# Window attention, convolution and MLP block on one core: values as fp32 weights with ones columns, one K/Q array for both score passes, unrolled code, a new order on every engine, long matmuls as two 64-column halves

## The reference, cut to what matters

```python
xn = layernorm(xw, g, b)                       # per token over 96 channels
q, k, v = split(xn @ qkv_w.T + qkv_b)          # 12 heads of 8
attn = softmax(q * SCALE @ k.T + bias)         # 49 x 49, per window and head
seq = x + (attn @ v) @ proj_w.T + proj_b       # back in image order
bn = batchnorm(depthwise_conv3x3(seq))         # inference constants
out = bn + gelu(bn @ w1.T + b1) @ w2.T + b2    # 96 -> 384 -> 96
```

## Time and profile before

| what | value |
|---|---|
| three runs | 4437.77, 4467.01, 4476.71 us |
| median | 4467.01 us |
| span of the profiled execution (its own time) | 4483.3 us, 16 us above the median |
| busy in it: TensorE, VectorE, ScalarE, GpSimd | 4149.9, 4035.2, 3540.7, 1813.2 us |
| instructions | 143736 |
| DMA issued by SP | 329.89 MB |

### The profile page before, as it was taken

One profiled execution on the slowest core, in us unless ns is written; L12 is line 12 of the kernel. 1 busy time (PEld: TensorE's weight loads), 2 busy tenths in 40 slices (PEclk: granted clock), 3 DMA queues, 4 the chain that ended last, 5 costly groups with the idle time before them and its releaser, 6 DMA issues.

```text
span 4483.3 us, 143736 instructions
## 1 busy us (share of the span) xinstructions
PE 4149.9 (93%) x51980; PEld 2703.3 (60%) x51980; DVE 4035.2 (90%) x7480; ACT 3540.7 (79%) x5891; POOL 1813.2 (40%) x1559
## 2 busy tenths in 40 slices
PE   4999999999999999999999999999999999999998
PEld 2666666666666666666666666666666666666665
DVE  6799999889999999998999899999999998988997
ACT  2688887878878788878888788788788888787886
POOL 3334444444343434434443434344343443434442
PEclk9899999999999999999999999999999999999998
DMA  1222222222222222222222222222222222222221
GB/s 48 69 76 81 77 78 76 78 78 81 77 77 77 77 78 80 76 78 75 80 81 76 79 76 78 76 81 78 76 78 77 80 76 80 75 79 77 80 79 41
DMA packets 363523, 340.69 MB, mean 76 GB/s; under 512 B 67200, under 2 KB 362561, under 8 KB 362708
## 3 DMA queue, kind: packets, MB, share of 16 engines
q1 hardware_dynamic: 362708, 329.89, 25.5%
HBM read 39.48 MB, written 38.54 MB: 17 GB/s over the span
## 4 chain that ended last, share of the span: by engine, by line
DVE 38%; issue 26%; PE 18%; SPq 11%; DMA 4%; ACT 2%; DVEq 1%; ACTq 0%; POOL 0%; POOLq 0%
DVE s L808 11%; DVE mx L777 6%; SPq L278 5%; DVE rec L790 4%; DMA q_bd<-ql 3%; DVE vl L844 3%; DVE on L794 3%; SPq L276 2%; PE a_ps L517 2%; DVE y L838 2%; SPq L319 2%; PE st_ps L368 2%; DVE kl L817 2%; DVE ol L856 2%; PE st_ps L362 2%
## 5 line engine op out<-in xcount | busy, mean ns | idle before, releaser
L680 POOL TENSOR_TENSOR pl<-p,ph 128x588 f16<-128x588 f32 x1024 | 1349.1, 1317 | 1890.5 <-ACT ph L584 1890.5
L808 DVE SCALAR_TENSOR_TENSOR s<-ximg,cols,s 96x392 f32<-96x392 f32 x2048 | 1610.6, 786 | 98.2 <-issue 71.4
L777 DVE TENSOR_REDUCE mx<-sm_ps 128x12 f16<-128x588 f32 x1024 | 780.8, 763 | 126.1 <-PE sm_ps L383 118.5
L581 ACT ACTIVATE p<-st_ps 128x588 f32<-128x588 f32 x1024 | 673.4, 658 | 184.9 <-PE st_ps L368 162.6
L584 ACT ACTIVATE ph<-st_ps 128x588 f16<-128x588 f32 x1024 | 681.9, 666 | 0.0
L517 PE MATMUL a_ps<-g,w_s 128*96 128x392 f32 x1536 | 618.2, 512 | 0.0
L336 PE MATMUL o_ps<-vh,ph 128*128 128x36 f16 x6144 | 559.9, 182 | 1.8 <-POOL pl L680 1.7
L337 PE MATMUL o_ps<-vl,ph 128*128 128x36 f16 x6144 | 551.0, 180 | 0.0
L338 PE MATMUL o_ps<-vh,pl 128*128 128x36 f16 x6144 | 551.0, 180 | 0.0
L336 PEld LDWEIGHTS o_ps<-vh,ph 128*128 128x128 f16 x6144 | 487.3, 96 | 53.2 <-POOL pl L680 2.3
L368 PE MATMUL st_ps<-q_bd,k_st 113*64 113x98 f16 x12288 | 484.3, 214 | 34.0 <-issue 34.0
(11 more groups left out here) (131 smaller groups left out, 8347.0 us busy)
## 6 DMA issues: line engine op xcount, KB each, us to landing
q_st<-qm SPq DMA_DIRECT2D x512, 96.0 KB
q_bd<-qh SPq DMA_DIRECT2D x1024, 48.0 KB
k_st<-kh SPq DMA_DIRECT2D x512, 96.0 KB
x_sb<-in_x SPq DMA_DIRECT2D x256, 147.0 KB, 2.3
out<-y SPq DMA_DIRECT2D x256, 147.0 KB, 2.4
k_bd<-kh SPq DMA_DIRECT2D x512, 48.0 KB
k_st<-kl SPq DMA_DIRECT2D x256, 96.0 KB
q_bd<-ql SPq DMA_DIRECT2D x512, 48.0 KB
```

The lines of the kernel that those rows point to most:

```text
L581: af(p32[:, q % 2, :, :].rearrange("p (b h) n -> p b h n", b=2), src, ACT.Exp)
L680: tt(pl[:, p % 2, :, 0:TOK], p32[:, p % 2, :, :], ph[:, p % 2, :, 0:TOK], ALU.subtract).then_inc(pl_done, 1)
L777: v.tensor_reduce(mx[:, (st[1] - lag) % 2, :, p].rearrange("p (b h) -> p b h", b=2), sm_ps[:, :, 0:HALF].rearrange("p b (h n) -> p b h n", ...
L808: v.scalar_tensor_tensor(acc, image_rows(st, lag, k // 3, k % 3), cw_c[:, k:k + 1], acc, ALU.mult, ALU.add)\
```

## The change

- All steps are written out (`for s in range(STEPS)`, 266 of them); every semaphore target is a constant. Many semaphores are split by pass.
- `k_all` and `q_all` (128 rows: rows 0 to 31 hold the three terms of a head's 8 channels, every fourth row a term; the rows behind them, and three spare ones, are one-hot for the keys in `k_all` against the bias's high and low part in `q_all`; row 127 takes the maximum) serve both passes. The maximum pass uses rows 0 to 126. SP issues nine DMAs a step.
- Both passes: 24 matmuls of 49 columns per pair of windows, each with 49 weight columns in one 64-partition half. L362, `qm`, `k_bd`, `q_st` are gone.
- One exponential, fp32. `values_times_p` has V as fp32 weights: 32 columns per head and pair of windows, column 4d+0 and 4d+1 the value for either window, 4d+2 and 4d+3 ones, so that the output has O and the sums, channels first, in a 32-partition group. V is written by one VectorE product with a 0/1 table (`half_c`).
- ScalarE copies O out; GpSimd issues four DMAs that gather every fourth partition into `ox`; ScalarE turns the sums into 1/sum as exp(-ln sum); VectorE multiplies; the projection is fp32 with its bias added in `image_sum`. Transposes, `oh` and `ol` are gone.
- `wide`: every matmul with over 64 output channels is issued as two, each with 64 weight columns (96 channels are padded to 128).

```diff
-                for b in range(2):
-                    mm(st_ps[:, b, 0:HALF], hot2[:, :, :].rearrange("p a b -> p (a b)"), lo_l[:, b * HALF:(b + 1) * HALF],
-                       start=True, stop=False, skip_group_check=True)
-                for j in range(NJ):
+                for h in range(HEADS):
                     for w in range(2):
-                        n = (2 * q + w) * WP
-                        c0 = j % (NJ // 2) * 2 * TOK
-                        last = mm(st_ps[64 * w:64 * w + 64, j // (NJ // 2), c0:c0 + 2 * TOK], k_st[:, r, j, n:n + WP],
-                                  q_bd[:, r, 2 * j:2 * j + 2, n:n + TOK], start=False, stop=True, skip_group_check=True)
+                        n, c0 = (2 * p + w) * WP, h % HH * TOK
+                        last = mm(st_ps[64 * w:64 * w + TOK, h // HH, c0:c0 + TOK], k_all[:, r, h, n:n + TOK],
+                                  q_all[:, r, h, n:n + TOK], start=True, stop=True)
...
+            def wide(o, w, m, start=True, stop=True):
+                for h in range(2):
+                    last = mm(o[64 * h:64 * h + 64], w[:, 64 * h:64 * h + 64], m, start=start, stop=stop)
+                return last
...
+                for g3 in range(NG):
+                    for c4 in range(4):
+                        h, at = 4 * g3 + c4, (2 * g3 + p % 2) * TOK
+                        last = mm(o_ps[32 * c4:32 * c4 + 32, at:at + TOK], v32[:, c % 2, h, p, :], p32[:, p, h, :], start=True, stop=True)
...
+            def to_channels(c):
...
+                wait(pool, proj_done, c - 2)
+                wait(pool, o_done[0], c)
+                wait(pool, o_done[1], c)
...
+                for x4 in range(4):
+                    nc.gpsimd.dma_start(ox[:, c % 2, x4, :], o_sb[x4::4, c % 2, :, :]).then_inc(o_in[c % 2], 16)
```

More of the change, by code:

```diff
@@ L325, in _, with load, term @@
-            run(sp, step)
+            def load(c):
+                if not real(c):
+                    return
+                wait(sp, sum_done, c - CPI)
+                at = c % CPI * CT
+                sp.dma_start(x_sb[:, at:at + CT], dram_rows(x, c)).then_inc(x_in[c % 8], 16)
+            def term(t, n, part, done, c):
+                if not real(c):
+                    return
+                wait(sp, done, c)
+                sp.dma_start(t[n:TERMS:4, c % 4, :, :], part[:, c % 2, :]).then_inc(exp_in[c % 4], 16)
@@ new lines, in store @@
+            def store(c):
+                if not real(c):
+                    return
+                wait(sp, y_done, c)
+                sp.dma_start(dram_rows(out, c), y[0:C, c % 2, :]).then_inc(stored[c % 2], 16)
+            for s in range(STEPS):
+                first_term(k_all, 1, kl, kl_done, s - 3)
+                load(s)
+                term(k_all, 0, kh, kh_done, s - 3)
+                term(q_all, 0, qh, qh_done, s - 3)
+                term(q_all, 1, qh, qh_done, s - 3)
+                term(q_all, 2, ql, ql_done, s - 3)
+                term(k_all, 2, kh, kh_done, s - 3)
+                store(s - 10)
+                maximum_row(s - 4)
@@ L457, in values, with projection @@
                 last.then_inc(v_done, 1)
-            def channels_first(st):
-                if not real(st, 4):
+            def projection(c):
+                if not real(c):
                     return
-                wait(pe, norm_done, st, 4, 4)
-                if real(st, 0):
-                    wait(pe, lnv_done, st, 0)
-                else:
-                    wait(pe, y_done, st, 8)
-                for n in range(NP):
-                    last = nc.tensor.transpose(a_ps[0:C, n * 128:(n + 1) * 128], on[:, n, :], eye_f[:, :])
-                last.then_inc(ot_ps_done, 1)
@@ L472, in projection @@
[L472 to L486 removed]
+                wait(pe, norm_done, c)
@@ new lines, in second @@
+            def second(c, k):
+                if not real(c):
+                    return
+                wait(pe, g_done[k], c)
+                if k == 1:
+                    free(pe, (g_done[2], c+0), (sum_done, c+2), (lnv_done, c+7), (y_done, c-1))
+                wide(a_ps[0:128, 0:CT], w2_s[:, k, :], g[:, k, :], start=k == 1, stop=k == 2).then_inc(s_done[k], 1)
+            for s in range(STEPS):
+                hidden(s - 8, 0)
+                hidden(s - 8, 1)
+                maxima_rows(s - 3)
+                hidden(s - 8, 2)
+                max_scores(s - 2, 0)
+                exp_scores(s - 4, 3)
+                values_times_p(s - 4, 1)
+                values_times_p(s - 4, 0)
+                second(s - 8, 1)
+                keys(s - 1)
+                max_scores(s - 2, 1)
+                second(s - 8, 0)
+                second(s - 8, 2)
+                queries(s - 1)
+                exp_scores(s - 3, 0)
+                values_times_p(s - 4, 2)
+                values_times_p(s - 4, 3)
+                max_scores(s - 2, 2)
+                centred(s)
+                values(s - 2)
+                exp_scores(s - 3, 1)
+                variance(s)
+                max_scores(s - 2, 3)
+                exp_scores(s - 3, 2)
+                projection(s - 5)
@@ L893 @@
     w_qkv, b_qkv, w_proj = a(L0_conv_qkv_w), a(L0_conv_qkv_b), a(L0_conv_proj_w).T
+    low = np.zeros((ROWS, 1), np.float32)
+    for row, key, n in LOW:
+        low[row:row + n] = -1.0
+    half = np.zeros((128, 2), np.float32)
+    for w in range(2):
+        half[64 * w:64 * w + TOK, w] = 1 / UP
     col = lambda v: a(v).reshape(C, 1)
@@ L910 @@
         "eye": np.eye(128, dtype=np.float32),
+        "low": low, "half": half,
     }
```

913 lines of the change are left out of this document (393 added, 520 removed).

## The result

The changed kernel takes 3539.8 us (median of 4 runs, 3533.4 to 3545.4) against 4471.9 for the one before on the same chip: 0.7918 of its time, with a 95% interval of 0.7885 to 0.7951. It is the number of rival D (3540), by coincidence: D had TensorE without waits, and it does wait.

The account below looks back on a forecast made before the run. Neither TensorE nor VectorE alone was taken as the bound. From 4483.3 us: -180 loop, -485 steps (16.3 to 14.4 us), -15 fill, +10 short last steps, -16 to the median: 3795 us, range 3610 to 3980.

Parts of the forecast that it names:

- rival D: TensorE runs its list without waits: 13.4 us a step, 3540 us in all; chance 0.05.
- Loop: Writing out all steps removes 30 back edges of 6.0 us: 180 us less, with straight code priced at 0.
- rival C: Gain only partly had, through weight loads (44 ns a pair), fetch or late results: 15.2 to 16.3 us a step; chance 0.17.
- TensorE, P times V: 48 fp32 matmuls a step at about 47 ns plus four shape changes: 2.65 us, range 2.25 to 4.3, against 1.83.
- fp32 halves: Long fp32 matmuls on TensorE, issued as two overlapping halves, still cost 0.66 us each, with results 0.33 us later.
- projection: On TensorE, two fp32 matmuls of 196 columns without transposes: 0.75 us a step against 1.92.
- GpSimd's issues: GpSimd issues four DMAs itself, at 1.0 us each, out of 0.7 to 2.5.
- what I cannot see: Allowance of 0.4 us a step for unseen costs, added to 13.3 of TensorE work and 0.7 of waits.
- Rival A: The fp32 halves on TensorE do not overlap: 21.9 us a step, about 5780 us in all; chance 0.08.
- B: GpSimd's transfers hold ScalarE, deciding the step from 1.46 us an issue; up to 18.2 us a step, about 4790; chance 0.11.
- VectorE and ScalarE: Busy time a step falls from 15.96 to 12.1 us on VectorE and from 13.9 to 10.9 on ScalarE.
- SP: SP issues nine DMAs for 18; nothing waited long for it, so no gain was counted there.

Follow-up runs that it names:

- the fastest version: Changed kernel with SP issuing the keys' terms first and the load behind all terms, and O's four transfers moved from GpSimd to SP: 3397.6 us, 0.7601.

## Why the prediction was wrong

*Loop:* right, 168 for 180, in a run of its own. The price of straight code was put at nothing, with the rest in rival C. For the list before that holds. In the changed kernel's denser list TensorE stands 0.54 us a step in issue, most of it in holes that go with the fetching of instructions (last section).

*TensorE, P times V:* the term that was mis-sized. It took 2.65 us a step, out of 2.25 to 4.3, "about 47 ns a matmul, plus four changes of shape"; it is 1.32, under the lower end. The working gave the overlap to one record of each matmul, by the halves of L368. There are four column groups, and the order turns through all four. Its 41 ns a record held (43 within a group), but four groups do this at once: 22 ns a matmul, 27 with the change of shape. The bound was no bound, since it let at most two groups overlap. 1.33 x 255 = 339 us, more than the whole miss.

*fp32 halves, projection, GpSimd's issues:* the times are right or better (0.66 to 0.68; 0.69 for 0.75; 0.57 us for 1.0). The order of the halves was read wrongly: they do not follow one another shifted by one record, both start together (7 ns apart), so the results are not 0.33 later. The 0.3 us a step named for that stands in the sum only as far as "what I cannot see" holds it. Rival A is refuted by the timeline, B by 9.6 us of waits in the whole run, C's pairs of 44 ns by 27; C's other half, fetch, did take its 0.5 us a step.

*VectorE and ScalarE:* right, 11.85 for 12.1 and 11.24 for 10.9. Taps are 619 ns for 0.62.

*SP:* the step that was missing. "Nothing waited long for SP, so nothing is gained there" asked only what SP gives back, not what hangs on it afterwards. In the changed kernel six issues of 0.7 us and the load stand between the keys and the next maximum pass, and a landing of 3.0 to 3.6 behind them. With 3.9 us ahead of them this closes at 12.9, more than TensorE's 11.8. The sum held 1.1 us of waits, 0.7 of them named (ScalarE's exponential, the logarithm) and 0.4 "for what I cannot see"; it was 13.29 - 11.82 = 1.5. In the trace 1.05 of that are gaps of over 0.1 us: 0.41 for the keys' transfer, 0.54 in issue, 0.09 ahead of the projection, and next to nothing for the exponential.

*Sum:* steps of 13.29 for 14.4 are -283 us, the fill is 141 for 168, -27; the short last steps take some of it back, and so do the 16 us taken off for the profiled execution, which here lies 4 us under the median. The reasons for the direction held. The size came out of two errors of opposite sign: a list 1.5 us a step too long, 1.33 of it in a term whose own range was too narrow, and waits 0.4 too short.

## What to carry to other kernels

When a change adds copies or transfers between the place where something is made and the place of its next use, draw that chain round to its own start and add it up (issues in their order, landing, work on both sides); compare it with every engine's list, however idle the queue looks before. An order on the issue queue costs nothing to change: here, to put the terms that the next step waits for ahead of the load was worth 108 us, and another queue for four other transfers 34 more. And when work turns through four parallel parts of an engine, the lower bound of its cost is the cost in one part divided by four, until a row shows that fewer overlap.

## What the runs showed of the hardware

**Column groups.** Twenty-four fp32 matmuls of 49 columns with 32 weight columns take 0.66 us when they turn through the four column groups, and 1.20 us when three in a row go to one group. Within a group a record takes 43 ns in both; the difference is how many groups run at once, four or two.

**Landing.** The last of the six terms lands 3.0 us after its issue's end where GpSimd's first transfer is issued together with it (the kernel after, the second layer's product twice), and 1.9 to 2.0 where that comes 0.6 us later or more (the order of P times V, the centred product twice, keys first); medians from the packets. In all of these SP sends a load or a store right behind, so 2.0 is not the landing of a transfer alone. That GpSimd's transfers are the reason is read from this order of the runs; none left them out. The Trainium skill, "SBUF — State Buffer", Who interferes with whom, has GpSimd's descriptors starve while VectorE holds the shared port. GpSimd's 1024 issues took 0.56 to 0.73 us each, and no such thing shows; but the instructions that the page names for it (copies, casts, tensor_scalar) are not those that ran beside them in the step shown (products, maxima, sums), so this is no test of it.

**Holes without a releaser.** TensorE stands still for up to 2.0 us (2.3 with two key terms on GpSimd) at places where it waits for nothing shown. From the chain of the kernel after:

```profile
2022.85 0.38 PE b_ps L250 x18
2023.23 1.62 issue
2024.85 0.31 PE b_ps L250 x6
```

Counted from the records between 300 and 3200 us, gaps over 0.8 us that are put to issue: 71 (86 us) in the kernel after, 75 (93) with the keys first, 76 (93) in the fastest version, all of them at the 194th or 195th instruction of a block of 256 in TensorE's list; 19 (20) when the fastest has a product more, and 4 (6) with whole products and the keys first. The page of the kernel after has 742 packets with 12.16 MB on the instruction queue, 16.4 KB each, and 742 blocks of 256 are TensorE's instructions. In these three runs every hole ends 1.1 to 1.7 us after the end of such a packet; of moments taken at random some 13% do. So TensorE waits there for its next block of instructions, as far as records can tell: no run changed the fetching alone. The runs do show that these holes pay for added work: 169 us of a product more arrived as 91, and the holes shrank by 73 in 2900 us. By the same account whole products would have cost some 260 us instead of 157 (an estimate). The Trainium skill, "Runtime: NRT & Kernel Launch", Instruction fetch mechanics, has blocks of 256 instructions, 16 KiB, which agrees with the packets, and has their fetching mostly hidden; in a list with some 730 matmuls and weight loads in 12.87 us it was not. It is not the straight code by itself: the kernel before, written out, has none of these gaps; its steps hold some 400 of these instructions in 16 us.
